# A new step order in the first feed-forward layer, and shorter stacks in the first attention

## The reference

```python
def _L0_attn_ref(x, w_qkv, b_qkv, w_out, b_out):      # first attention
    q, k, v = split_heads of x @ w_qkv + b_qkv         # 16 heads of 16
    a = jnp.einsum('bhsd,bhtd->bhst', q, k)
    a = (a + causal_mask) / np.sqrt(HEAD_DIM)
    a = jax.nn.softmax(a, axis=-1)
    z = jnp.einsum('bhst,bhtd->bhsd', a, v)
    return z @ w_out + b_out

# second half of each of the two layers (feed-forward, HID = 682)
h = shift_token(x)
h = (h - mu) / jnp.sqrt(var + 1e-05) * lg + lb
h = h @ w1 + b1
a, g = jnp.split(h, 2, axis=-1)
h = a * jax.nn.gelu(g, approximate=False)
x = x + h @ w2 + b2
```

## Time and profile before

| what | value |
|---|---|
| median of three runs | 1941.19 us |
| profiled execution, its own time | 1938.0 us |
| its span, first to last instruction | 1936.5 us |
| PE busy | 1763.7 us, 91% |
| DVE, ACT, POOL busy | 1128.9, 974.2, 934.8 us |
| mean granted clock of PE | 0.936 |

### The profile page before, as it was taken

How to read it: one execution, slowest core, us unless ns; L and a number is a source line. 1 busy time by engine, 2 the same in 40 slices (tenths; PEclk the granted TensorE clock), 3 DMA queues, 4 the chain that set the end, 5 groups by cost and what they waited for, 6 DMA issues and landing times. The chain is left out here.

```text
span 1936.5 us, 42847 instructions
## 1 busy us (share of the span) xinstructions
PE 1763.7 (91%) x14072; PEld 1337.1 (69%) x14072; DVE 1128.9 (58%) x2827; ACT 974.2 (50%) x1898; POOL 934.8 (48%) x923
## 2 busy tenths in 40 slices
PE   5889989898669999999969999689999999879997
PEld 3556655565347777777758888567777777678886
DVE  5566766666467667666633333666666776325554
ACT  2655655555336555555543444345555655434443
POOL 3355445555346555555632333445556665325444
PEclk7898999998779999999988999889999999979998
DMA  4333343434010010010021222200000000212221
GB/s 146 111 115 105 108 136 113 122 113 131 23 35 12 33 32 32 32 32 22 0 89 55 65 65 90 63 12 33 32 32 0 32 32 22 78 52 79 87 87 44
DMA packets 103736, 121.29 MB, mean 63 GB/s; under 512 B 23386, under 2 KB 75780, under 8 KB 103684
## 3 DMA queue, kind: packets, MB, share of 16 engines
q1 hardware_dynamic: 96772, 95.45, 16.2%
q0 software_dynamic: 6912, 25.17, 3.7%
HBM read 82.55 MB, written 37.77 MB: 62 GB/s over the span
## 5 line engine op out<-in xcount | busy, mean ns | idle before, releaser
L470 DVE TENSOR_REDUCE a_negm<-a_x 128x2 f32<-128x256 f32 (+3 forms) x256 | 201.8, 814 | 127.2 <-PE a_x L596 125.2
L430 ACT ACTIVATE a_PT<-a_c 128x384 f32<-128x384 f32 (+1 forms) x384 | 183.7, 523 | 137.4 <-PE a_c L635 84.7
L868 POOL TENSOR_TENSOR work<-work 128x512 f32<-128x512 f32 x128 | 164.8, 1289 | 151.8 <-DVE work L1018 150.8
L1036 DVE CUSTOM_DVE_ANT_0 l_x<-l_x,window 128x256 f32<-128x256 f32 (+1 forms) x512 | 184.7, 425 | 31.6 <-PE l_x L1133 31.6
L1438 POOL TENSOR_TENSOR m_hid_lo<-m_hid,m_hid_hi 128x512 fp32r<-128x512 f32 x80 | 102.9, 1296 | 183.8 <-ACT m_hid_hi L1492 183.6
L1543 DVE SCALAR_TENSOR_TENSOR m_hid<-m_a,mw_b,m_gate 128x512 f32<-128x512 f32 x96 | 72.0, 750 | 196.9 <-ACT m_gate L1481 168.8
L1067 PE MATMUL l_f<-w_hi,tails 128*128 128x512 f32 x384 | 168.5, 439 | 14.0 <-DVE work L1018 10.9
L951 ACT ACTIVATE l_PT<-l_c 128x512 f32<-128x512 f32 (+1 forms) x256 | 125.4, 542 | 87.4 <-PE l_c L1173 83.8
L1068 PE MATMUL l_f<-w_hi,tails 128*128 128x512 f32 x384 | 154.8, 403 | 0.0
L1069 PE MATMUL l_f<-w_lo,tails 128*128 128x512 f32 x384 | 154.2, 402 | 0.0
L882 POOL TENSOR_TENSOR l_PS<-l_PT 128x768 f32<-128x768 f32 x64 | 119.9, 1874 | 58.6 <-ACT l_PT L951 58.6
(11 more groups left out here) (241 smaller groups left out, 5101.0 us busy)
## 6 DMA issues: line engine op xcount, KB each, us to landing
a_Q<-qk_parts SPq DMA_DIRECT2D x192, 64.0 KB, 2.1
a_K<-qk_parts SPq DMA_DIRECT2D x192, 64.0 KB, 2.1
qk_parts<-a_qk_hi SPq DMA_DIRECT2D x32, 256.0 KB, 2.1
qk_parts<-a_qk_lo SPq DMA_DIRECT2D x32, 256.0 KB, 2.2
after_attn<-rows_out POOLq DMA_DIRECT2D x16, 512.0 KB, 5.3
xin<-after_attn SPq DMA_DIRECT2D x32, 256.0 KB, 3.1
m_xr<-after_attn SPq DMA_DIRECT2D x16, 512.0 KB, 4.0
xin<-in_L_attn_x SPq DMA_DIRECT2D x8, 512.0 KB, 3.6
```

The lines of the kernel that those rows point to most:

```text
L430: nc.scalar.activation(PT[:, p // PG % 2, 2 * (p % PG) + hh, QOFF[t]:QOFF[t] + nq], SC[hh][:, 0:nq], ACT.Exp, scale=AD ** -0.5).then_inc(e ...
L470: dve.tensor_reduce(negm[:, q, 2 * p:2 * p + 2], MX[i % 2][:, :, 0:nk], AX.X, ALU.max, negate=True).then_inc(max_done, 1)
L868: pool.tensor_tensor(t1[:, par, w, :], t1[:, par, w, :], t2[:, par, w, :], ALU.add)\
L1036: m = dve.tensor_tensor_reduce(out=o, in0=o, in1=mask, scale=-1.0, scalar=-NEG, op0=ALU.add, op1=ALU.min, accum_out=negm[:, q + t, p // 2, ...
```

## The change

1. In the feed-forward part of layer 0 another table of steps is used; layer 1 keeps the table of before, now named LAST_STEPS.
2. In the first attention the row of the maximum moves from 63 to 48 (SLOTS), the two products run over 48 and 49 rows instead of 63 and 64, and the zeroing of Q's rows 32 to 63 and 96 to 127 is gone, with the two counts that the loads waited for.

```diff
-        ODD, SHIFT = 64, 63
+        ODD, SLOTS = 64, 48
...
                         if i == 0 and isinstance(b, int):
                             sp.wait_ge(stacks_set, 2)
-                            sp.wait_ge(v_set, 5)
+                            sp.wait_ge(v_set, 3)
...
-                            at = ODD * hh + SHIFT
+                            at = ODD * hh + SLOTS
...
-                            for at in (32, ODD + 32):
-                                dve.memset(Q[at:at + 32, :, 0:S].bitcast(F32), 0.0).then_inc(v_set, 1)
...
-                            rows = slice(ODD * hh, ODD * hh + SHIFT)
+                            rows = slice(ODD * hh, ODD * hh + SLOTS)
...
-                            rows = slice(ODD * hh, ODD * hh + ODD)
+                            rows = slice(ODD * hh, ODD * hh + SLOTS + 1)
...
         STEPS = [s.rsplit(":", 1) for s in """
+            f_in:0 f_n:0 w1:2 f_m:0 w1:3 w2:0 h:2 f_t:0 w1:4 xr:0 h:3 w1:5 h:4 w2:1 w2:2 w2:3 f_te:0 h:5 f_w1:0 w2:4
+            w2:5 y:0 fin:0 f_w1:1 f_h:0 f_h:1""".split()]
+        LAST_STEPS = [s.rsplit(":", 1) for s in """
             f_n:0 w1:2 h:2 f_m:0 w2:0 w1:3 w2:1 w1:4 h:3 h:4 f_in:0 xr:0 f_t:0 w1:5 w2:2 h:5 w2:3 w2:4 f_te:0 w2:5
             y:0 f_w1:0 f_h:0 f_w1:1 fin:0 f_h:1""".split()]
-        STEPS = [(name, int(i)) for name, i in STEPS]
+        STEPS = [(name, int(i)) for name, i in (LAST_STEPS if last else STEPS)]
```

## The result

The changed kernel has a median of 1961.94 us over four runs (1959.16 to 1963.94), the kernel before in the same comparison 1941.56: 20.4 us slower, a ratio of 1.0105 with a 95% interval of 1.0085 to 1.0126. The forecast was 1951.7, 10.1 us slower. The sign was right and the time lies in the wide range of 1941 to 1963, but outside the forecast's own 1948 to 1957, and the change is twice the forecast one.

A forecast was written before the change was run, and what follows sets the result against it. PE was taken to bound layer 0's feed-forward stage, without idle time; 0 + 10.5 + 0 = +10.5 us on the profiled 1938.0 gave 1948.5, plus 3.2 for the median: 1951.7, own range 1948 to 1957, wide range 1941 to 1963.

The forecast's parts named there:

- (a), the hole: Layer 0 feed-forward loop: PE waits 1.50 us before the transposes in each of 7 turns, +10.5 us.
- R1: Layer 0 feed-forward loop: PE's new waits also bring the lower clock, 11.2 us if every turn, 1963 us; chance 0.14.
- (a), the rest of the table: Layer 0 feed-forward loop: the other moved steps are covered and cost nothing.
- (b), the memset pair: First 19 us, DVE: removing 2 x 3.47 us gains 0, since the loads wait for the DMA.
- (c), the rows: First attention: matmuls over 48 and 49 rows take as long as over 63 and 64, so 0.
- R2: First attention: fewer rows shift the clock; one more low stretch per batch 1964 us (slow half), one fewer 1939; chance 0.06.
- R3: Layer 0 feed-forward loop: ACT's m_hn comes in time, PE does not wait, 1941 us, no change; chance 0.12.
- R4: First attention: matmul time falls with the rows, saving 26.7 us, 1925 us in all; chance 0.04.

The follow-up runs named there:

- the version without the hole: Kernel before with the new table in layer 0, its transposes moved one place later, behind w1:4; second comparison 1937.62 us against 1941.85, ratio 0.9976.

## Why the prediction was right and wrong

- **(a), the hole: right in place and size.** Every time in the chain came out within 0.03 us, the turn grew by 1.51 for 1.50, and moving the one step made the stage 10.4 us shorter, for the 10.5 of the sum. The idle time shown for the group, 8.8 us, is just under the 9 to 12 foretold, as it counts from modelled ends. The clock stayed at 1.00 in that loop in the profile, with a wait and eight transposes in each of seven turns, so R1 did not happen.
- **(a), the rest of the table at nothing: off by about 4 us.** By the second comparison of the version without the hole the other moves give 4.2 us (1.7 to 7.6 by the interval), and what explains them was not found.
- **(b), the memset pair at 0: right** as far as the runs can tell. Keeping it gave 12.7 us instead of 11.4, within the spread.
- **(c), the rows at 0: this is the step that failed.** The argument was that 106 and 128 rows take 280 ns alike. That holds for the duration of a matmul at a given clock, and the equal least durations after confirm it. It says nothing on the clock itself, which the rows also move: both row counts of the earlier trace rows ran at 1.00. The group's mean did not stay at 414 ns, it rose to 435. The rows cost 11.4 us by themselves (7.8 to 14.4 by the interval), and 12.5 on top of the table without the hole.
- **R2 is what happened, with a chance of 0.06.** Its slow half had the mechanism, the clock of the first attention moved by its fewer rows, and the price, 12.8 us on top of the forecast with the hole in it: 1964, for 1961.94 measured. Two things were wrong in it. The words that nothing in the trace speaks for either sign overlooked that the clock of that stage was unsettled, 0.90 with PE 89% busy, while the local attention had 0.96 and the feed-forward loop 1.00; that told of a risk, though not of its sign. And the price came from a guess of one more low stretch in each batch, so its nearness is in part luck. The parts measured alone, 11.4 for the rows and 6.6 for the table (10.4 for the hole less about 4), make 18.0; the change is 20.4, and the spread of the runs covers the rest.
- **R3 and R4** are out: the hole is there, and no matmul got shorter with fewer rows.

## What to carry to other kernels

Where the mean granted clock of a stage lies between its two levels, cost an edit not only by the duration of its instructions: here rows taken out of the array cost clock although no matmul got longer, and zero rows that looked like waste paid for themselves. Equal durations of two shapes answer one question, the clock another; a term is at nothing only when both are. Where PE has no idle time, place each step by when the chain that feeds it is ready, from rows of the trace. Here one step set one place too early cost 10.4 us, and the working had said 10.5. Judge a shift of the clock by all executions and not by one profile: with nothing changed in the first attention its end moved by 9 us from one profile to another.

## What the runs showed of the hardware

- Single dense streams of 512-column matmuls held 2.4 GHz with 52, 56, 60 and 64 rows, and fell to 1.2 GHz with 50, 48, 40, 32, 24 and 16, though PE was busy without a gap in all of them (one execution each, 48 rows in three).
- Dense pairs of 48 rows from partitions 0 and 64 ran side by side (0.115 us for each matmul) and held 2.4 GHz.
- The 15 rows that the change removed carried zeros on one side of the product and ones on the other. They added nothing to the result. Without them in the first product alone, with nothing else changed, the kernel was 8.1 us slower and the clock lower in the profile, 0.86 instead of 0.90.
- Eleven 128-row matmuls in each of seven batches, put into two waits of the first attention, took PE's idle time from 47.2 to 32.4 us and did not raise the clock beyond its spread (0.89 and 0.90).
